# Block-sparse attention on one NeuronCore: the first pair of heads starts its scores after six steps of row maxima instead of twelve

## The reference, cut to what matters

```
inner      = einsum('bhlqd,bhlkd->bhlqk', mq, exp_k) * scale       # own and neighbouring blocks
first_band = einsum('bhlqd,bhkd->bhlqk', mq, kb[:, :, 0]) * scale
last_band  = einsum('bhlqd,bhkd->bhlqk', mq, kb[:, :, -1]) * scale
aw = softmax(concatenate([first_band, inner, last_band], -1), -1)
```

## Time and profile before

| | |
|---|---|
| runs | 1834.7, 1838.37, 1841.88 us; median 1838.37 |
| profiled execution, its own time | 1834.21 us |
| its span | 1832.4 us |
| PE busy | 1627.5 us (89%) |
| DVE busy | 1164.6 us (64%) |
| ACT busy | 912.7 us (50%) |
| POOL busy | 618.3 us (34%) |

### The profile page before, as it was taken

One profiled execution on the slowest core, in us unless ns is written; L12 is line 12 of the kernel. 1 busy time (PEld: TensorE's weight loads), 2 busy tenths in 40 slices (PEclk: granted clock), 3 DMA queues, 4 the chain that ended last, 5 costly groups with the idle time before them and its releaser, 6 DMA issues. The chain is left out here.

```text
span 1832.4 us, 35552 instructions
## 1 busy us (share of the span) xinstructions
PE 1627.5 (89%) x12958; PEld 1364.5 (74%) x12958; DVE 1164.6 (64%) x2478; ACT 912.7 (50%) x2007; POOL 618.3 (34%) x585
## 2 busy tenths in 40 slices
PE   8889999999996977999997798899974699999990
PEld 6677777777774866788886354699963699999990
DVE  6767667677786684755554687667647555555543
ACT  4317877777876543533332575444420444444434
POOL 3430000000443753777774243333310332222221
PEclk9999999999998999999999899999985799999995
DMA  8891333323425601344443630001123224233315
GB/s 279 301 153 43 66 76 84 70 63 63 124 42 186 229 35 52 59 71 72 75 67 59 158 80 1 1 24 47 47 89 118 44 85 98 85 98 84 84 17 183
DMA packets 146392, 165.42 MB, mean 90 GB/s; under 512 B 78970, under 2 KB 118000, under 8 KB 146160
## 3 DMA queue, kind: packets, MB, share of 16 engines
q1 hardware_dynamic: 109376, 110.94, 21.7%
q0 software_dynamic: 28544, 47.35, 12.1%
q10 hardware_dynamic: 8304, 4.85, 1.5%
HBM read 109.47 MB, written 61.08 MB: 93 GB/s over the span
## 5 line engine op out<-in xcount | busy, mean ns | idle before, releaser
L889 DVE TENSOR_REDUCE att_neg_max<-att_m_ps 128x1 f32<-128x320 f32 x496 | 216.2, 487 | 102.7 <-PE att_m_ps L615 100.2
L2033 PE MATMUL silu_h_ps<-silu_xT,silu_w_part 128*128 128x320 f32 x1536 | 236.6, 312 | 0.9 <-DVE silu_xT L2129 0.9
L2033 PEld LDWEIGHTS silu_h_ps<-silu_xT,silu_w_part 128*128 128x128 f32 x1536 | 227.0, 189 | 2.1 <-DVE silu_xT L2129 1.3
L615 PE MATMUL att_m_ps<-att_k,att_q 96*128 96x384 f32 x496 | 182.0, 381 | 7.3 <-DMA att_q<-qk 5.0
L1998 POOL DMA_INDIRECT summed<-silu_y,all_table x40 | 63.8, 1596 | 256.7 <-DVE silu_y L2169 153.8
L1749 POOL DMA_INDIRECT part<-all_xT,all_table x72 | 119.1, 1654 | 60.7 <-DVE all_xT L1880 48.7
L1028 POOL DMA_DIRECT2D att_q<-att_max_row x40 | 20.4, 509 | 336.7 <-DVE att_max_row L897 336.6
L615 PEld LDWEIGHTS att_m_ps<-att_k,att_q 96*128 96x128 f32 x496 | 94.1, 190 | 38.1 <-issue 18.0
L2045 PE MATMUL silu_y_ps<-silu_w_part,silu_h_part 128*128 128x256 f32 x960 | 116.5, 283 | 2.2 <-DVE silu_w_part L2145 2.2
L2045 PEld LDWEIGHTS silu_y_ps<-silu_w_part,silu_h_part 128*128 128x128 f32 x960 | 115.9, 192 | 2.5 <-DVE silu_w_part L2145 2.5
L1785 PE MATMUL gelu_h_ps<-gelu_wu_part,gelu_xT 128*128 x402 | 110.2, 409 | 2.6 <-DVE gelu_wu_part L1887 2.5
(11 more groups left out here) (335 smaller groups left out, 3993.1 us busy)
## 6 DMA issues: line engine op xcount, KB each, us to landing
experts_w<-in_dram SPq DMA_DIRECT2D x24, 1024.0 KB, 8.5
qk<-qkv_part POOLq DMA_DIRECT2D x32, 512.0 KB, 4.6
att_k<-qk SPq DMA_DIRECT2D x192, 64.0 KB, 2.3
att_q<-qk SPq DMA_DIRECT2D x168, 64.0 KB, 3.4
v<-qkv_v POOLq DMA_DIRECT2D x8, 544.0 KB, 6.2
att_v<-v SPq DMA_DIRECT2D x8, 544.0 KB, 4.7
qkv_x<-in_dram SPq DMA_DIRECT2D x8, 512.0 KB, 4.9
raw_wu<-in_dram SPq DMA_DIRECT2D x2, 2048.0 KB, 13.7
```

Source lines behind the costliest of these rows:

```text
L615: nc.tensor.matmul(bank[:, 0:2 * LOCAL].rearrange("p (a n) -> p a n", a=2), q[b][0:MROW, x, :], local_and_global(b, x), start=True, stop=T ...
L889: ins = nc.vector.tensor_reduce(neg_max[b][:, x - 1:x], bank[:, 0:LOCAL + 2 * BLK], AX.X, ALU.max, negate=True)
L2033: mm = nc.tensor.matmul(h_ps[u % 2][a][:, :], w12_part[f % RING][wp][:, a, k, :], xT[s][xp][:, k, rows], start=(i == 0), stop=(i == 3 * KD ...
```

## The change

`FIRST_LEAD` = 6 steps of maxima stand ahead of the first scores instead of 12. In the first twelve steps of the loop the maxima are taken up faster than one step per step: `maxima_until(g)` grows by one in even g and by two in odd g, until the lead is 12 again at g = 11. From g = 12 on the order is as before.

```
-    LEAD = 12
+    LEAD, FIRST_LEAD = 12, 6
...
+        def maxima_until(g):
+            return min(FIRST_LEAD + g + 1 + min((g + 1) // 2, LEAD - FIRST_LEAD), TOTAL)
+
         def maxima_of(g):
-            return divmod(g + LEAD, STEPS) if g + LEAD < TOTAL else None
+            return [(n // STEPS, n % STEPS, at) for n in range(maxima_until(g - 1), maxima_until(g))
+                    for at in range(len(M[n % STEPS]))]
...
-            for n in range(LEAD):
+            for n in range(FIRST_LEAD):
                 for at in range(len(M[n])):
                     maxima(0, n, at)
                     idle_products(1)
             for g in range(TOTAL):
                 ms = maxima_of(g)
-                units = len(M[ms[1]]) if ms is not None else 0
-                for at in range(max(units, 3)):
-                    if at < units:
-                        maxima(*ms, at)
+                for at in range(max(len(ms), 3)):
+                    if at < len(ms):
+                        maxima(*ms[at])
                     if at < 3:
                         scores(g, at)
```

More of the change, by code:

```diff
@@ L962, in _ @@
             for g in range(TOTAL):
[L963 to L966, removed]
+                for unit in maxima_of(g):
+                    maximum(*unit)
                 if g in INVERT_BESIDE:
```

## The result

| | before | after |
|---|---|---|
| median of the runs | 1838.73 us (5 runs, 1834.7 to 1841.88) | 1848.41 us (5 runs, 1846.59 to 1850.12) |
| ratio | | 1.0045, 95% interval 1.0027 to 1.0063 |
| profiled execution | 1834.21 us | 1849.25 us |

The forecast was 1848.0 us. The ratio makes 8.3 us (5.0 to 11.6) of the difference, the two medians 9.7 us.

A forecast was written before the change was run, and what follows sets the result against it. The start was taken as bound by transfers, the first row of maxima landing last, and the loop nearly by PE. Terms -0.3 + 8.4 + 1.5 = +9.6 us gave 1848.0 us on the median, range 1839 to 1856 us.

The forecast's parts named there:

- What bounds the start: Ahead of the loop: the landing of the first row of maxima, at about 127.05 us, sets the start, not the maxima.
- -0.3 us: Gain from work removed ahead of the loop: start at 127.2 instead of 127.5 us; bounds 0 and 7.5 us gain.
- the rival's early row: Ahead of the loop: the row lands after 2.4 us, sum +2.4 us, 1840.8 us; chance 0.16.
- The surplus units: Loop steps 0 to 11: units added between scores and transpose, with waits for three banks, cost +8.4 us; bounds 4.3 and 12.1.
- the rival of PE's price alone: In the loop: row late, but DVE catches up, so units cost 4.3 us; sum +5.5, 1843.9 us; chance 0.14.
- The clock: First loop steps: PE at half clock behind a stall of some 16 us costs +1.5 us; bounds 0 and 3.
- the rival "the clock stays low": First loop steps: PE remains at 1.2 GHz for two or three steps; about +14 us, 1852.4 us; chance 0.04.
- The sum: Whole execution: +9.6 us, giving 1843.8 us for the profiled execution and 1848.0 us on the median.
- These signs: In the profile: execution of 1843.8 us, and L845 of g = 12 at about 168 us instead of 158.4.

The follow-up runs named there:

- the hold: SP's loads for the second pair held until the first row of maxima has landed: on the change 1840.42 us, on the kernel before 1835.93 us.
- cheap: The change with DVE's reductions of the first pair's blocks 21 to 62 over 32 columns instead of 320; 1845.89 us in one run.
- spread: The change with PE's surplus units of steps 1 to 11 spread over each step, the fifth row's transpose behind the values; 1853.42 us.
- lead8: The change with FIRST_LEAD 8 instead of 6; 1848.45 us, ratio 1.0045.
- after_warm_over: The change with 105 unread matmuls in the stall ahead of the first scores, ending beyond the landing of the row; 1851.88 us.
- after_warm: The change with 70 unread matmuls in the stall ahead of the first scores; 1849.03 us, ratio 1.0057.
- eight steps and the early loads: The change with FIRST_LEAD 8, second pair's loads held until the first row landed, first pair's values loaded behind the second chunk of keys; 1834.85 us.

## Why the prediction was right

- *What bounds the start.* Right, and shown: PE stood 19.11 us for the row, and the hold alone moved the start by 10.6 us. The start was not at 127.2 but 131.4 us: the row was issued 1.8 us later and flew 2.4 us longer. Its flight varies, 9.5 and 13.2 us in the two profiles of before and 11.9 in the change. Before varies too (127.5 and 133.8 us), there by the landing of the third chunk of queries: in all four twelve-step profiles the first score matmul follows that landing by 8.0 to 9.1 us and doesn't wait for the row. So "-0.3 us" stands on the mean of few profiles: +0.7 from 130.6 to 131.4, and over the four plain kernels with six or eight steps whose start isn't moved on purpose (after, cheap, spread, lead8: 131.4, 128.4, 128.7, 130.5) -0.9. That the mean comes so near to -0.3 us is in part luck. No profile with the second pair's loads in front shows the rival's early row. The hold makes that row on purpose (start 120.8 us), and the time, 1840.42 us, is near the rival's 1840.8.
- *The surplus units.* +8.4 us was worked out, 8.5 measured at full clock (after_warm_over). Step by step: g = 3 3.97 (2.45 + 1.5), g = 5 4.08 (3.95), g = 7 3.43 (3.35), g = 9 3.98 (3.75), g = 11 3.68 (3.75). That is also what rules out the rival of PE's price alone, 4.3 us. The division between PE's price and the bank waits was off: 1.0 and 0.5 us for five units, against 0.9 and 0.6; for the steps with c units it wasn't measured.
- *The clock.* The mechanism was right and its size wrong: 1.5 us forecast, 3.5 measured, above my bound of 3. The price was taken from the earlier trace rows, where half clock lasted 3.8 us; in the loop it lasted some 11 us with PE busy, through steps 0 and 1. So the condition of the rival "the clock stays low", to which I gave 0.04, came true, at less than its price: it had 2.45 us more in each of two or three steps, and the two steps together cost 3.5 us, 2.0 above the forecast.
- *The sum.* From start to step 12 the price is 42.83 - 30.86 = 12.0 us against 9.9 forecast. For the execution I had forecast 1843.8 us, and it took 1849.25; step 12 was to come at about 168 us and came at 174.2. These signs missed by 5 to 6 us, 4.2 of them by the start and 2.0 by the clock. With a start 0.7 us later or 0.9 earlier the price would be 11.1 to 12.7 us, above the 9.7 of the medians and at the end of the interval of the ratio (5.0 to 11.6). So the median came within 0.5 us of the forecast partly by luck: too low a clock price met something that takes 1.4 to 3 us away. The part behind step 12 took 1669.4 to 1677.3 us over all profiles, so a mean there can hide that much; it isn't settled. The range was loosely added up: +12 and 3 us on the median give 1853.4, and only the low-clock rival comes near its 1856; the early row less 3 us gives 1837.8, not 1839.

## What to carry to other kernels

Before a run-up is shortened, look for what else the first step of the loop waits for: work ahead of a transfer that lands last is free, and in the loop it has a price on the engine that is full. A trace shows one landing of such a transfer; profile the kernel twice before a term is built on its time. To let a loop start earlier, take traffic from in front of the transfer that gates it, which here gained 5 us with twelve steps and 8 us with six, with no engine's compute order touched.

## What the runs showed of the hardware that was not expected

- A transfer of 8 KB that POOL issued took 7.6 to 13.2 us to land where the DMA share was above 1.0, and 2.3 and 3.0 us in the kernels with the hold alone. The Trainium skill ("DMA: Bandwidth & Descriptors", section "Anatomy of one DMA — SWDGE (gpsimd) path") gives such a transfer a fixed 2.0 us. Only the 2.3 and 3.0 us come near it.
- PE's granted clock fell to half right behind a stall of 2.1 us that followed 15.8 us of unbroken matmuls at full clock (after_warm), and it stayed there for some 10 us, to about 141 us, with PE 3.40 of 3.40 and 3.29 of 3.40 us busy. In the earlier trace rows it had been back after 3.8 us, on a stretch with PE 3.62 of 3.80 us busy, and in the second profile of before after some 5.9 us. With eight steps and the early loads it stayed at half for over 12 us. What sets these apart isn't shown.
